# Norm and scan steps inside the scans' stage, and a unit's maxima taken by halves of the keys

## What is computed

```
layer 1: two Mamba-2 scans of layernorm(x), one forward, one over the reversed sequence, added
  z, xBC, dt = x @ in_w.T            # 512 + 640 + 8 columns per direction
  dt = softplus(dt + dt_bias);  A = -exp(A_log)
  x, B, C = silu(causal conv over 4 taps of xBC + conv_b)
  S = S * exp(dt A) + (dt x) B       # 8 heads of 64, state 64
  y = (S C + Dp x) * silu(z);  y = y * rsqrt(mean(y*y) + eps) * norm_w;  out = y @ out_w.T
layer 2: attention (16 heads of 16, softmax over all 2048 keys, scores scaled by
  2 * sigmoid of a projection of q), gate, residual and norm, top-2 router, the expert with the
  higher index of 8, weighted and added, norm
```

## Time and profile before

| | us |
|---|---|
| median of three runs | 2585.23 (2582.33 to 2591.15) |
| the profiled execution | 2587.86 |
| its span, first to last instruction | 2586.0 |
| block 1 (norm, steps) | 0 to 68.1 |
| block 2 (scans) | 68.3 to about 726.6 |
| block 3 (residual, values) | 728.6 to 784.1 |
| block 4 (attention) | 784.5 to about 2212 |
| blocks 5 and 6 | from there to 2586 |

### The profile page before, as it was taken

How to read it: one execution, slowest core, us unless ns; L and a number is a source line. 1 busy time by engine, 2 the same in 40 slices (tenths; PEclk the granted TensorE clock), 3 DMA queues, 4 the chain that set the end, 5 groups by cost and what they waited for, 6 DMA issues and landing times. The chain is left out here.

```text
span 2586.0 us, 45326 instructions
## 1 busy us (share of the span) xinstructions
PE 2443.0 (94%) x16377; PEld 1085.6 (42%) x16377; DVE 2092.5 (81%) x4149; ACT 1799.0 (70%) x2367; POOL 996.6 (39%) x1191
## 2 busy tenths in 40 slices
PE   6799999999867999999999999999999999897996
PEld 6366666666543223232223222222223322474554
DVE  4577777888766998999889999999899995283877
ACT  2587787677621778788778787787787878552664
POOL 1377777888961121222121221121211101254564
PEclk9899999999988999999999999999999999887998
DMA  2222232233241030404004012040040000225883
GB/s 91 90 82 83 81 98 86 90 98 97 70 126 35 14 62 14 62 14 63 1 13 63 13 32 32 14 62 2 13 62 2 2 2 2 73 75 200 281 284 111
DMA packets 111811, 174.14 MB, mean 67 GB/s; under 512 B 19290, under 2 KB 86514, under 8 KB 106452
## 3 DMA queue, kind: packets, MB, share of 16 engines
q1 hardware_dynamic: 103684, 155.20, 22.8%
q0 software_dynamic: 6016, 14.49, 1.5%
q10 hardware_dynamic: 1888, 1.56, 0.2%
HBM read 145.28 MB, written 27.02 MB: 67 GB/s over the span
## 5 line engine op out<-in xcount | busy, mean ns | idle before, releaser
L1597 DVE TENSOR_REDUCE max_part<-round_psum 128x1 f32<-128x512 f32 x2048 | 1269.7, 684 | 104.1 <-PE round_psum L1511 99.1
L1563 ACT ACTIVATE p_exp<-score_psum 128x1024 f32<-128x1024 f32 x1024 | 993.4, 1022 | 216.2 <-PE score_psum L1498 210.7
L1511 PE MATMUL round_psum<-k_stack,q_stack 64*128 64x512 bf16 x2048 | 706.4, 385 | 20.2 <-DVE pv_psum L1589 8.8
L1489 PE MATMUL score_psum<-q_stack,k_stack 64*128 64x512 bf16 x2048 | 599.7, 379 | 0.9 <-ACT p_exp L1563 0.2
L1498 PE MATMUL score_psum<-q_stack,k_stack 35*128 35x512 bf16 x2048 | 595.2, 378 | 0.3 <-DMA q_stack<-max_rows 0.3
L1539 PE MATMUL pv_psum<-p_exp,values 128*17 128x512 f32 x4096 | 539.5, 598 | 0.0
L1511 PEld LDWEIGHTS round_psum<-k_stack,q_stack 64*128 64x128 bf16 x2048 | 189.4, 94 | 610.7 <-DVE max_part L1597 511.5
L637 PE MATMUL rot<-tokens_t,w_in 128*128 128x512 f32 x576 | 273.2, 607 | 17.3 <-DVE bc_conv L789 13.9
L1498 PEld LDWEIGHTS score_psum<-q_stack,k_stack 35*128 35x128 bf16 x2048 | 188.8, 94 | 116.8 <-DMA q_stack<-max_rows 0.9
L1631 POOL TENSOR_TENSOR rden<-pv_out,minus_one 128x16 f32<-128x16 f32 x32 | 92.9, 2902 | 359.0 <-ACT pv_out L1581 356.7
L1489 PEld LDWEIGHTS score_psum<-q_stack,k_stack 64*128 64x128 bf16 x2048 | 139.5, 94 | 59.1 <-ACT p_exp L1563 26.4
(11 more groups left out here) (282 smaller groups left out, 3581.0 us busy)
## 6 DMA issues: line engine op xcount, KB each, us to landing
expert_w<-in_expert_w SPq DMA_DIRECT2D x39, 1028.0 KB, 5.3
cum_rows_in<-cum_rows SPq DMA_DIRECT2D x64, 512.0 KB, 3.9
cum_pairs_in<-cum_rows SPq DMA_DIRECT2D x120, 128.0 KB, 3.8
qk_rows<-qk_parts SPq DMA_DIRECT2D x64, 192.0 KB, 3.1
q_stack<-qk_rows SPq DMA_DIRECT2D x84, 128.0 KB, 8.1
k_stack<-qk_rows SPq DMA_DIRECT2D x84, 128.0 KB, 9.1
token_rows<-tokens SPq DMA_DIRECT2D x12, 512.0 KB, 4.2
x_in<-in_x SPq DMA_DIRECT2D x8, 512.0 KB, 8.8
```

The costliest lines, as they stand in the source:

```text
L1489: nc.tensor.matmul(ebank[i // 2][:, i % 2, :], ks[rows, n % 2, plane, k * P:(k + 1) * P], qs[rows, n % 2, plane, q * BLK:(q + 1) * BLK], s ...
L1511: nc.tensor.matmul(bank[step][:, :], qs[rows, n % 2, plane, at:at + P], ks[rows, n % 2, plane, keys * BLK:(keys + 1) * BLK], start=True, s ...
L1563: nc.scalar.activation(pt[:, (k * 2 + pair) % 4, :, :], ebank[pair][:, :, :], ACT.Exp).then_inc(*exped.up(u, k, pair))
L1597: nc.vector.tensor_reduce(mx[:, c * HG + h, keys:keys + 1], bank[step][:, :], AX_X, ALU.max).then_inc(*maxed.up(u, k, i))
```

## The change

1. `norm_and_steps` goes. A class `Steps` holds its tiles as views of buffers of the scans' stage (x in `tokens`, the normalized blocks in `M`, the steps' work in `cum`, `cum2` and `xdt`; the PSUM parts in the banks `xt`, `gb`, `up`, `yp` and `rows_bank`). Its work is words of the engines' orders in `mamba`, in a new table `BEGIN`, which replaces the fixed beginning of `mamba_order`.
2. SP's queue starts with x blocks 0 to 2, the projection weights, one channel table, x blocks 3 to 7, the other table, w_out; then the save of the sums; then it waits for `eto` before the loads of the sums.
3. New waits follow from the shared buffers: the first tile of block 0 and of block 1 on PE waits for the transposed tokens, ACT and DVE wait for the channel table at the first tile, `across` on PE and x_w on POOL wait for `etot` at chunk 0, the gate waits for the last z tile of its block.
4. On DVE the bias of the backward half comes before that of the forward half; the scaling of w_out is two words, `w_out0` and `w_out1`, later in the order. A mask table that nothing reads is no longer loaded.
5. `stack1` leaves block 3; its loads are issued at the start of attention. A unit's maxima go first over all heads and chunks with the first half of the keys, then with the second. For the first unit PE waits at step 0 for the first half's stacks only, and at step 8 for the second half's.

```diff
+BEGIN = {
+    "PE": "x_turn0 x_turn1 tile4 x_steps0 x_turn2 tile0 x_steps1 tile1 x_turn3 x_steps2 x_turn4 tile2 x_steps3 "
+          "tile5 tile3 x_turn5 x_steps4 x_turn6 x_steps5 x_turn7 x_steps6 x_steps7 x_flip tile6 tile7 x_cum "
+          "x_cum_t tile8 products0 next4",
+    "ACT": "x_turn0 tile4 x_turn1 tile0 x_turn2 tile1 x_turn3 x_turn4 tile2 x_turn5 tile5 x_turn6 tile3 x_turn7 "
+           "x_exp x_log tile6 silu_x silu_z tile7 x_eto next4 skip decays0 tile8 decays1 spread1",
+    "DVE": "x_stats0 halo x_stats1 x_turn0 x_stats2 x_turn1 x_stats3 x_turn2 x_stats4 x_turn3 tile4 x_stats5 "
+           "tile0 x_turn4 tile1 x_stats6 x_turn5 x_stats7 x_turn6 x_turn7 tile2 x_raw w_out0 x_plus_one tile3 "
+           "x_dt x_cum w_out1 products0 next4 m0",
+    "POOL": "x_stats0 x_stats1 x_stats2 x_stats3 x_stats4 x_stats5 x_stats6 x_stats7 decays0 decays1 products0",
+}
...
+    for word in BEGIN[engine].split():
+        what, at = word.rstrip("012345678"), word.lstrip("abcdefghijklmnopqrstuvwxyz_")
+        if what == "tile":
+            yield "project", 0, int(at)
+        elif what == "next":
+            yield from tile(1, int(at))
+        else:
+            yield what, 0, int(at or 0)
...
+    T = Steps(sems, acc, M, cum, cum2, xdt, (xt, gb, up), rows_bank, up, yp, up, rows_bank)
...
         @block.sync
         def _(sp_):
+            for b in range(NBLK):
+                c = slice(b * CPB, (b + 1) * CPB)
+                nc.sync.dma_start(T.x[:, c, :], xv[:, c, :]).then_inc(*T.x_load[b].up(0))
+                if b == 2:
+                    nc.sync.dma_start(w_in[:, :, :], io["w_in0"]).then_inc(*loaded["w_in"].up(0))
+                    nc.sync.dma_start(chan[0][:, :], io["chan0"]).then_inc(*loaded["chan0"].up(0))
+            nc.sync.dma_start(chan[1][:, :], io["chan1"]).then_inc(*loaded["chan1"].up(0))
             for d in range(2):
                 nc.sync.dma_start(w_out[d][:, :, :], io[f"w_out{d}"]).then_inc(*w_out_load[d].up(0))
+            sp_.wait_ge(*T.on_vector.at("cum_t"))
+            nc.sync.dma_start(cum_dram.rearrange("(a p) t -> p a t", p=P),
+                              T.cumT.rearrange("p d k t -> p (d k) t")).then_inc(*loaded["cum_rows"].up(0))
             sp_.wait_ge(*loaded["cum_rows"].at(0))
+            sp_.wait_ge(*T.on_scalar.at("eto"))
...
                 if what == "project":
+                    if (n, c) in first_tiles:
+                        pe.wait_ge(*T.x_t.at(block_at(n), KD - 1))
...
+                    if q == 0:
+                        pe.wait_ge(*T.on_scalar.at("etot"))
...
                     if q % CPB == 0:
                         ve.wait_ge(*z_ready.at(n))
+                        ve.wait_ge(*z_act.at(n, z_done[n]))
...
-    "SP": "weights0 load4 weights1 fill load7 load5 keep4 load6 save0 keep5 stack0 save1 stack1 keep6 keep7",
+    "SP": "weights0 load4 weights1 fill load7 load5 keep4 load6 save0 keep5 stack0 save1 keep6 keep7",
...
 def max_at(k, i):
-    p, rest = divmod(k, 2 * CPB)
-    return 2 * p + i % 2, rest // 2, 2 * (rest % 2) + i // 2
+    half, rest = divmod(k, KT // 2)
+    p, c = divmod(rest, CPB)
+    return 2 * p + i % 2, c, 2 * half + i // 2
...
+    for t in range(TERMS):
+        yield "stack", 0, 1, t
     for t in range(-LEAD, total + 4):
...
-                    if q == 0 and k == 0 and i == 0:
+                    if (u, k, i) == (0, 0, 0):
+                        pe.wait_ge(*S.first_stacked.all())
+                    if q == 0 and k == (0 if n else KT // 2) and i == 0:
                         pe.wait_ge(*S.stacked[n % 2].at(n, 1, TERMS - 1, "k", 1))
```

The words that begin with `x_` call four new functions, one for each engine, with the old instructions. The parts that differ from before:

```diff
+class Steps:
+    def __init__(self, sems, acc, M, cum, cum2, xdt, banks, dtp, flip, cump, totp, cum_t):
+        n = NCH * NH
+        self.x = acc
+        self.xn = M.rearrange("p two (c d) -> p two c d", d=D)
+        four = cum.rearrange("p two (s n) -> p (two s) n", n=2 * n)
+        self.raw, self.tmp, self.lg, self.da = (four[:, i, :].rearrange("p (d n) -> p d n", d=2) for i in range(4))
...
+def steps_on_vector(nc, ve, K, own, T, sp, what, b):
...
+    if what == "raw":
+        ve.wait_ge(*T.dt_load.all())
+        ve.wait_ge(*T.summed.at("dt"))
+        nc.vector.tensor_tensor(g3(T.tmp, 1), T.dtp[:, :, 1, :], bias[1], ALU.add).then_inc(*T.on_vector.up("tmp"))
+        nc.vector.tensor_tensor(g3(T.raw, 0), T.dtp[:, :, 0, :], bias[0], ALU.add).then_inc(*own.up())
```

More of the change, by code:

```diff
@@ new lines, in steps_on_scalar @@
+def steps_on_scalar(nc, act, T, xnT, sp, what, b):
+    if what == "turn":
+        for k in range(KD):
+            act.wait_ge(*T.turned.at(b, k))
+            nc.scalar.copy(xnT[:, k, b * BLK:(b + 1) * BLK], T.bank(b, k)[:, :]).then_inc(*T.x_t.up(b, k))
+    if what == "exp":
+        act.wait_ge(*T.on_vector.at("softplus_in"))
+        nc.scalar.activation(T.tmp, T.tmp, ACT.Exp).then_inc(*T.on_scalar.up("exp"))
+    if what == "log":
+        act.wait_ge(*T.on_vector.at("plus_one"))
+        nc.scalar.activation(T.lg, T.tmp, ACT.Ln).then_inc(*T.on_scalar.up("log"))
+        act.wait_ge(*T.dt_load.all())
+        nc.scalar.activation(T.neg_a, T.a_log, ACT.Exp).then_inc(*T.on_scalar.up("a"))
+    if what == "eto":
+        act.wait_ge(*T.on_vector.at("rest"))
+        nc.scalar.activation(sp["eto"][:, :, :], T.rest, ACT.Exp).then_inc(*T.on_scalar.up("eto"))
+        for r in range(2):
+            o = slice(r * NST, (r + 1) * NST)
+            e = nc.scalar.activation(sp["etot"][o, :, :].rearrange("p d (g j) -> p (d g) j", j=NH // 2),
+                                     T.totp.rearrange("p (a j r) -> p a j r", j=NH // 2, r=2)[o, :, :, r], ACT.Exp)
+        e.then_inc(*T.on_scalar.up("etot"))
@@ new lines, in steps_on_vector @@
+    if what == "plus_one":
+        ve.wait_ge(*T.on_scalar.at("exp"))
+        nc.vector.tensor_scalar_add(T.tmp, T.tmp, 1.0).then_inc(*T.on_vector.up("plus_one"))
+    if what == "dt":
+        ve.wait_ge(*T.on_scalar.at("a"))
+        nc.vector.tensor_scalar_mul(T.neg_a, T.neg_a, -1.0).then_inc(*own.up())
+        nc.vector.scalar_tensor_tensor(sp["dt"][:, :, :], T.raw, 0.0, T.lg, ALU.max, ALU.add).then_inc(*own.up())
+        ve.wait_ge(*own.last())
+        for d in range(2):
+            v = nc.vector.tensor_tensor(g3(T.da, d), g3(sp["dt"], d), neg[d], ALU.mult)
+        v.then_inc(*T.on_vector.up("da"))
@@ L387, in chunk @@
         return [(what, q // CPB, q)] if 0 <= q < NQ else []
-    x_tiles, z_tiles = [[("project", 0, c) for c in some] for some in ((4, 0, 1, 2, 3), (5, 6, 7, 8))]
-    here = {what for part in STEPS[engine] for what in part.split()}
-    if engine == "ACT":
-        yield from chunk("decays", 0)
-    yield from x_tiles
-    if engine == "ACT":
-        yield "silu_x", 0, 0
-    yield from z_tiles
-    if engine == "ACT":
-        yield from [("silu_z", 0, 0), ("skip", 0, 0)]
-    for what, q in (("decays", 0), ("products", 0), ("m", 0), ("decays", 1), ("spread", 1)):
-        if what in here and not (engine == "ACT" and q == 0):
-            yield from chunk(what, q)
-    yield from tile(1, 4)
+    for word in BEGIN[engine].split():
[6 more added lines that the diff above has]
+            yield what, 0, int(at or 0)
     for q in range(NQ + 2):
@@ L2390 @@
 C_WIDTH = _at
-C_KEPT = C_AT["mask"][0]
 def constants():
```

329 lines of the change are left out of this document (143 added, 186 removed).

## The result

The changed kernel takes **2541.65 us** (median of 4 runs, 2537.0 to 2547.66), the kernel before 2584.03 us (4 runs): ratio 0.9832, 95% interval 0.9803 to 0.9862. The direction and the two places were right; the size was not.

What follows compares the result with a forecast made beforehand. PE was busy nearly throughout, with DVE's recurrence pacing the scans and PE or the maxima attention. The start's 16 us and the seam's 5.8 us, 21.8 us off the median 2585.2, gave 2563.4 us; range 2551 to 2576 us.

Steps and rivals of the forecast that it cites:

- The clock of the merged stage: PE's turns, steps and tiles at the start: slow until inside tiles 5 and 3, steps end at 66.5 us.
- All fast from the end of tile 4 ... 48 us: Merged start: fast end of the working, steps end at 48 us, where DVE would hold it near 50.
- clock high early: Rival, merged start: clock high from tile 0 or 1 on, steps end 60.7, 2554 us; chance 0.13.
- The sentence on the Trainium skill: Merged start: transposes don't count as clock activity, so turns stay low; as first rival 2572 us, chance 0.17.
- From the steps' end to the state: Start, save and load of sums to first recurrence state: 30 us taken, 28 by the load's way.
- a second way through ACT's queue: Start: next4 and skip stand ahead of the first decays on ACT, which makes 32 us from the steps' end.
- The loop: Scans' recurrence behind the start: the start's shift arrives whole, the next block takes 37 to 39 us.
- Given back: Rival: the scans' loop takes back the gain over its blocks, 2579 to 2585 us; chance 0.04.
- The seam's wait: Before attention: moving the stack loads brings PE's first maximum 5.8 us earlier, with 16 us of cover at step 8.
- The seam's clock: First maxima of attention: a fast PE saves at most 6 us; 0 was taken.
- The maxima by halves: Attention: same matmuls and reductions in another order, cost zero, 386 ns each.
- The slower rival: Attention: maxima and scoring read the same half of k_stack, at 20 ns more per matmul 2604 us; chance 0.05.

Runs made afterwards that it cites:

- e11: The changed kernel with only tile 4 left between turns and steps, the first block's other tiles after the steps; 2561.38 us beside 2585.34 (one run).
- e5: The changed kernel with the first block's projection tiles taken out from between turns and steps; 2568.04 us, ratio 0.9909.
- e7: The changed kernel with 36 dense matmuls on zeros on PE before the first turn; 2545.68 us, ratio 0.984.
- e14: The changed kernel with tiles 5 and 3 spread, 11 matmuls on zeros at the seam, and ACT's exponential and first decays moved earlier; 2544.34 us, ratio 0.9821.
- e12: The changed kernel itself, unaltered, profiled in one more execution; 2540.33 us.
- e4: The kernel before with the second half's stack loads issued in attention's block, but maxima in the old order; 2595.37 us, ratio 1.0028.
- e2: The kernel before with only the late second stack and the maxima by halves, on the old start; 2577.17 us, ratio 0.9957.
- e3: The kernel before with only the new order of maxima by halves, loads and waits as before; 2588.99 us, ratio 1.0002.
- e1: The changed kernel with everything of attention undone, so the merged start alone; 2550.04 us, ratio 0.9848.
- e6: The changed kernel with tile 5 moved behind turn 5 and tile 3 behind steps 5; 2545.16 us, ratio 0.9829.
- e10: The changed kernel with 11 matmuls on zeros behind PE's last work before attention; 2538.44 us, ratio 0.9819.
- e9: The changed kernel with 36 matmuls on zeros before the first turn, 8 after it, and ACT's exponential of the sums before the z tiles' silu; 2541.31 us, ratio 0.9822.
- e13: The kernel of e5 with 11 matmuls on zeros behind PE's last work before attention; 2562.16 us beside 2592.43 (one run).
- e8: The kernel before with 28 matmuls on zeros at the end of PE's stream in block 3, before attention; 2588.97 us, ratio 0.9998.

## Why the prediction was wrong

**The clock of the merged stage: wrong, the term of the sum that failed.** "So I take slow until inside that pair" put the rise at tiles 5 and 3, near 50 us; it came inside tile 4, at 19 us. The steps' end was 51.6 instead of 66.5 us, 14.9 of the 22.0 us by which the two profiled spans differ more than predicted. The step behind it was the reading of the earlier trace rows, where the clock rose 4 us into dense tiles: I took more than one tile to be needed. e11 shows that a single one is enough to raise it, e5 that without one it doesn't rise. The prediction had even worked out this case ("All fast from the end of tile 4 ... 48 us"; the slow tail from 43 us on adds the rest), but neither a rival nor the range went there: the rival "clock high early" took 60.7 us, and the low side of the range was built on its 2554 us. No working stands behind that 60.7: by the prediction's own prices a rise at the end of tile 0 gives about 52 us and one at the end of tile 1 about 55. DVE as a bound "near 50" was too high as well: the steps ended at 46.4 us in e7 and at 47.0 in e14. An end that the working itself gives belongs in the range.

The sentence on the Trainium skill (TensorE: Matmul & The Clock Gate, Part 4: transposes do not count as activity) leaned to the wrong side. The rows of e5 agree that turns and steps don't raise the clock. But they ran at the high level for some us once a tile had raised it: four transposes in 0.60 us instead of 1.06. "Doesn't raise" is not "stays low", and where the page says that the high level does not engage for transposes, these rows differ and decide. Nor are the 3.43 us that the prediction set beside the rule a row of transposes: they are short matmuls, on which that sentence says nothing.

**From the steps' end to the state: right in size, and by the first of its two ways.** 30 us predicted, 28.8 measured, with the new wait for `eto` (SP's load 4.0 us behind the save, 16.7 us behind the steps' end where 17.0 were worked out), the landing near 3.9 us and the decays as worked out. The 30 was a compromise between 28 and a second way through ACT's queue at 32. That one did not bind: ACT waited 1.38 us for POOL at the first decays. In the first way one term was short: from the mask product to the state took 2.9 us, not 1.6.

**The loop: right.** 37.8 us for the first block. 2.5 us of the shift went on the way to attention in the profiled execution, none in e12. "Given back" was no case.

**The seam's wait: right.** 5.8 us predicted, 5.9 measured; PE's first maximum 0.99 us behind ACT's last copy (predicted 1.13), stack loads from 748.72 us, and no wait for them at step 8. e4 shows what the late loads cost where the halves don't cover them.

**The seam's clock: wrong.** "I take 0, with the end at 6": 5.4 us measured, at the end that I didn't choose. The 3.69 us of the earlier trace rows were taken to show that 2.9 us would do the same damage; they show a slow tile, not how long the low level lasts. e2 has this term on the old start: 5.9 us of wait and 5.4 of lead-in.

**The maxima by halves: right.** 386 ns each as before, e3 at 1.0002. The slower rival is excluded.

In sum, 14.9 (steps' end) + 1.2 (chain) - 2.5 (loop) + 0.1 + 5.4 (lead-in) + 2.6 (attention and the stages behind it) = 21.7 us, beside the 22.0 us between the spans' shift of 43.8 and the 21.8 predicted; the 0.3 left is the start's gain of 16.3 us, rounded to 16. The clock's two terms, 14.9 and 5.4, are the miss; the loop's and the last term lie within the scatter from one execution to the next.

## What to carry to other kernels

Where PE has long runs of transposes and short matmuls at the low clock, look for dense matmuls that could stand among them: here six tiles among turns and steps cost no time at all, because much of what stood around them ran nearly twice as fast. A stage boundary with PE idle costs its idle time and then, perhaps, as much again in clock, so cost the two separately. Before a gain or a loss of 2 or 3 us is put down to an edit, look at the same stretch in a second execution: the stretch from the first state to the values' last copy differed by 9 us among these. When a working has a fast end, carry it into the range, even if one row speaks for the slow one.

## What the runs showed of the hardware

PE's clock rose within one projection tile, or at its very end, when that tile stood behind slow transposes (2.7 to 3.6 us for tile 4, in seven executions: the changed kernel, e1, e6, e10, e11, e12, e14). In turns and steps, without any idle time of PE, it fell 3 to 5 us behind the last tile in the changed kernel, e1, e6, e9, e11 and e12, but only 9 us behind it in e10, and in e7 the same turns and steps ran fast for 9.8 us, to their end. PE's waits of 1.93 us (e7), 0.92 us (e9) and 0.47 us (e6), inside such sparse work, were each followed by a slow tile, but each also came 3 to 4 us behind the last dense work, and a wait of 0.45 us in e14 was not; no run parts the two causes.

Behind 2.86 us of idle time at the seam (2.85 in e2) the clock was low for 3.4 us and the lead-in 45.1 us in six executions of five kernels, but low for 17.1 us with a lead-in of 49.9 us in e5 and e11; e13 differs from e5 only by the fill. With the idle time filled by matmuls on zeros down to 0.99 us the clock stayed high in e10, e13 and e14 (lead-in 44.0 us each); in e8, where 2.20 us were left, it fell for 13.6 us.
